# Two mixture-of-experts layers on one core: gate rows spread over the partitions by DMA instead of by a selector product on TensorE

## The reference

```python
def _L0_ffn_ref(...):
    shared = silu(xf @ Ws_up) @ Ws_down
    aff = xf @ centroids.T
    _, idx = top_k(aff + expert_biases, 8)
    w = sigmoid(take_along_axis(aff, idx, axis=1))
    w = w / (sum(w) + 1e-08)
    cw = zeros((T, E)).at[arange(T)[:, None], idx].add(w)   # the gates of layer 0
    h = silu(einsum('td,edf->etf', xf, W_up))
    y = einsum('etf,efd->etd', h, W_down)
    return shared + einsum('etd,te->td', y, cw)

def _L1_ffn_ref(...):
    probs = softmax(xf @ router_w.T)
    k_probs, k_idx = top_k(probs, 2)                        # normalised: the gates of layer 1
    # a token beyond an expert's capacity of int(1.25*N*2/8)+1 is dropped (gate 0)
    h = silu(buf @ w1); out = h @ w2                        # per expert
    return sum(out * gate) + x
```

## Time and profile before

| what | value |
|---|---|
| time, median of 3 runs | 1476.88 us (1471.17 to 1491.15) |
| the profiled execution's own time | 1489.87 us |
| its span | 1488.1 us |
| mean granted TensorE clock | 0.957 of full speed |
| PE busy | 1327.0 us, 89% |
| DVE busy | 1055.6 us, 71% |
| ACT busy | 949.4 us, 64% |
| POOL busy | 882.5 us, 59% |
| bytes read from HBM, written | 43.87 MB, 20.05 MB |

### The profile page before, as it was taken

How to read it: one execution, slowest core, us unless ns; L and a number is a source line. 1 busy time by engine, 2 the same in 40 slices (tenths; PEclk the granted TensorE clock), 3 DMA queues, 4 the chain that set the end, 5 groups by cost and what they waited for, 6 DMA issues and landing times. The chain is left out here.

```text
span 1488.1 us, 23328 instructions
## 1 busy us (share of the span) xinstructions
PE 1327.0 (89%) x6176; PEld 525.4 (35%) x6176; DVE 1055.6 (71%) x1843; ACT 949.4 (64%) x1732; POOL 882.5 (59%) x835
## 2 busy tenths in 40 slices
PE   2499898989889897599999999998999999999998
PEld 1223232322222221234444444443433444444443
DVE  6687887879787783577786786788878555455554
ACT  0055565757566576467767767766666777877776
POOL 2414342433433235467777777777777888878886
PEclk9997897989998899799999999999999999999999
DMA  2541523324252400431101001021110110001100
GB/s 60 86 68 41 78 56 57 74 38 91 35 83 51 65 5 9 124 94 29 40 9 40 27 29 40 8 85 34 57 37 8 37 29 26 13 21 29 30 7 8
DMA packets 92275, 65.36 MB, mean 44 GB/s; under 512 B 35786, under 2 KB 85900, under 8 KB 92172
## 3 DMA queue, kind: packets, MB, share of 16 engines
q1 hardware_dynamic: 91812, 63.91, 20.2%
q10 hardware_dynamic: 360, 0.30, 0.1%
HBM read 43.87 MB, written 20.05 MB: 43 GB/s over the span
## 5 line engine op out<-in xcount | busy, mean ns | idle before, releaser
L1266 POOL TENSOR_TENSOR m_hidl<-m_hid,m_hidh 128x512 f16<-128x512 f32 x520 | 613.3, 1185 | 212.2 <-ACT m_hidh L1311 188.8
L1534 DVE TENSOR_TENSOR m_hid<-m_silu,m_c 128x512 f32<-128x512 f32 x512 | 347.5, 684 | 247.7 <-ACT m_silu L1318 193.2
L588 ACT ACTIVATE a_probs<-a_score 128x512 f32<-128x512 f32 x512 | 293.8, 597 | 195.1 <-PE a_score L666 188.5
L1318 ACT ACTIVATE m_silu<-m_h 128x512 f32<-128x512 f32 x520 | 309.1, 595 | 131.1 <-PE m_h L1417 126.2
L1311 ACT ACTIVATE m_hidh<-m_hid 128x512 f16<-128x512 f32 x520 | 324.2, 624 | 90.8 <-DVE m_hid L1534 89.7
L762 DVE TENSOR_REDUCE a_mx<-a_mxps 128x2 f32<-128x1024 f32 x256 | 306.9, 1215 | 75.7 <-PE a_mxps L657 75.1
L666 PE MATMUL a_score<-a_qstack,a_kstack 74*128 74x512 bf16 x512 | 208.6, 412 | 21.3 <-DMA a_qstack<-a_mT 14.4
L657 PE MATMUL a_mxps<-a_kstack,a_qstack 72*128 72x512 bf16 x512 | 173.4, 424 | 43.2 <-DMA a_kstack<-t_parts 31.2
L1415 PE MATMUL m_h<-m_xh,m_wuh 128*128 128x512 f16 x520 | 198.8, 382 | 12.2 <-DMA m_rw<-rw 12.2
L1397 PE MATMUL m_y<-m_hidh,m_wdh 128*128 128x512 f16 x520 | 198.8, 382 | 2.5 <-ACT m_gT L1332 1.7
L1417 PE MATMUL m_h<-m_xh,m_wul 128*128 128x512 f16 x520 | 198.7, 382 | 0.0
(11 more groups left out here) (186 smaller groups left out, 1295.5 us busy)
## 6 DMA issues: line engine op xcount, KB each, us to landing
a_qstack<-t_parts SPq DMA_DIRECT2D x63, 128.0 KB
a_kstack<-t_parts SPq DMA_DIRECT2D x63, 128.0 KB
m_raw<-up SPq DMA_DIRECT2D x8, 512.0 KB, 3.9
m_raw<-down SPq DMA_DIRECT2D x8, 512.0 KB, 4.0
m_sT<-t_s SPq DMA_DIRECT2D x16, 256.0 KB, 3.4
t_parts<-a_qparts SPq DMA_DIRECT2D x24, 128.0 KB, 2.2
t_parts<-a_kparts SPq DMA_DIRECT2D x24, 128.0 KB, 2.3
a_xin<-x SPq DMA_DIRECT2D x8, 256.0 KB, 3.4
```

The costliest lines, as they stand in the source:

```text
L588: act.activation(probs[:, kt % 2, g, :], score[:, g % 2, :], ACT.Exp, scale=SCALE).then_inc(exp_done, 1)
L1266: pool.tensor_tensor(hidl[0:r0, k % r, :], hid[0:r0, k % r, :], hidh[0:r0, k % r, :], ALU.subtract).then_inc(lo_done, 1)
L1318: act.activation(silu[0:rows(q), k % RING[s.layer], :], hps[0:rows(q), k % 2, :], ACT.Silu, scale=1.0 / WS).then_inc(silu_done, 1)
L1534: dve.tensor_tensor(hid[:, k % r, :], silu[:, k % r, :], cps[:, (q // UPC[s.layer]) % 2, :], ALU.mult).then_inc(mul_done, 1)
```

## The change

The gates stay fp32 in DRAM (`cw0` 64 rows, `cw1` 8 rows). In both mixtures the selector product is gone: SP loads the row of each expert from DRAM straight to all partitions that need it, two rows per load (`GROUP`), into `gates`, a ring in SBUF of four groups, eight units in layer 0. In layer 0 a group takes two DMAs (one per half of the partitions, each 64 partitions x 2 rows x 2 KB) and serves two units; in layer 1 one DMA of 128 partitions x 2 rows serves eight units. DVE multiplies silu by the SBUF ring. A slot is refilled after its last product, also with the next stage's gates. The two PSUM banks that were `m_c` go to h, which has three in layer 0 and four in layer 1. The scaling by 64, which was the selector's, is in ACT's copy of cwT. The fp16 halves of the gates go (POOL L452, L455; DVE L1686, L1688), as do half the gate transposes in attention and three of four in layer 0; the selectors and the fp16 identity go as well. The loads of the weight chunks 4 to 9 move from ahead of the units into the units of the first stage.

```diff
+GROUP = 2
+GROUPS = UNITS // GROUP
+SLOTS = E1 // GROUP
+HBANKS = (3, 4)
...
-        cw = [sb(f"cw{p}", [P, TOK], F16) for p in range(2)]
+        gates = sb("gates", [P, SLOTS * GROUP, TOK])
...
-        cwhl = sb("cwhl", [P, TILES, 2, E1], F16)
-        cwT = sb("cwT", [2 * E1, TOK], F16)
-
-        hps = ctx.enter_context(nc.psum_tensor("m_h", [P, 2, 512], F32))
-        cps = ctx.enter_context(nc.psum_tensor("m_c", [P, 2, 512], F32))
+        cwT = sb("cwT", [TILES * E1, P])
+
+        hps = ctx.enter_context(nc.psum_tensor("m_h", [P, max(HBANKS), 512], F32))
...
+            def load_gates(s, g):
+
+                k = g % SLOTS
+                into = gates[:, GROUP * k:GROUP * k + GROUP, :]
+                if s.layer:
+                    sp.wait_ge(cw_out, Turn(0, s.i, s.p).n("cw_out", 16 * TILES))
+                    apart(sp)
+                    row = scratch["cw1"][GROUP * g:GROUP * g + GROUP, s.tokens()]
+                    sp.dma_start(into, row.unsqueeze(0).broadcast_to([P, GROUP, TOK])).then_inc(gate_in[k], 16)
+                    return
+                pair = scratch["cw0"].rearrange("(u a) t -> a u t", a=2)
+                for a in range(2):
+                    h = slice(a * (P // 2), a * (P // 2) + P // 2)
+                    row = pair[a, GROUP * g:GROUP * g + GROUP, s.tokens()]
+                    sp.dma_start(into[h], row.unsqueeze(0).broadcast_to([P // 2, GROUP, TOK])
+                                 ).then_inc(gate_in[k], 16)
...
             load_chunk(1)
+            for g in range(SLOTS):
+                load_gates(Turn(0, 0, 0), g)
             for dst, src in ((wg, "wg"), (bg, "bg"), (lnw, "lnw"), (lnb, "lnb"), (rw, "rw")):
...
             def unit(s, q):
+                if s.first() and q and 1 < (job_at(s, q - 1) or 0) < JOBS:
+
+                    j = job_at(s, q - 1) + 2
+                    sp.wait_ge(wsplit, 2 * (j - 1))
+                    load_chunk(j if j < JOBS else j + 1)
+                span = GROUP * (UPC[1] if s.layer else 1)
+                if q < UNITS and q % span == span - 1:
+
+                    g = q // span + SLOTS
+                    to = s if g < UNITS // span else s.following()
+                    if to:
+                        sp.wait_ge(mul_done, s.n("unit", q + 1))
+                        apart(sp)
+                        load_gates(to, g % (UNITS // span))
...
-                if not (s.first() and q < 2):
-                    pe.wait_ge(silu_done, s.n("unit", q - 1))
+                if not (s.first() and q < min(HBANKS)):
+                    pe.wait_ge(silu_done, s.n("unit", q - min(HBANKS) + 1))
...
-                if q < UNITS and q % UPC[n] == 0:
-                    c = q // UPC[n]
-                    if not (s.first() and c < 2):
-
-                        ago = (c - 1) * UPC[n] - (NQ[n] - UNITS if c < 2 else 0)
-                        if n and c < 2 and isinstance(s.i, int) and s.i == 0 and s.p == 0:
-                            ago = -1
-                        pe.wait_ge(mul_done, s.n("unit", ago))
-                    r = slice(0, 2 * (E0, E1)[n])
-                    pe.matmul(cps[:, c % 2, :], sel[n][:, c, :], cw[s.p][r], start=True, stop=True
-                              ).then_inc(c_done, 1)
...
-                if q < UNITS and q % UPC[s.layer] == 0:
-                    dve.wait_ge(c_done, s.n("c", q // UPC[s.layer] + 1))
+                if q < UNITS and q % (GROUP * UPC[s.layer]) == 0:
+                    g = q // (GROUP * UPC[s.layer])
+                    dve.wait_ge(gate_in[g % SLOTS], s.n("gate", 16 * (1 if s.layer else 2) * (g // SLOTS + 1)))
...
-                    dve.tensor_tensor(hid[:, k % r, :], silu[:, k % r, :], cps[:, (q // UPC[s.layer]) % 2, :],
+                    dve.tensor_tensor(hid[:, k % r, :], silu[:, k % r, :], gates[:, (q // UPC[s.layer]) % (SLOTS * GROUP), :],
                                       ALU.mult).then_inc(mul_done, 1)
```

More of the change, by code:

```diff
@@ L996, in back, with following @@
         return Turn(self.layer, self.i - 1, 1)
+    def following(self):
+        if self.p == 0:
+            return Turn(self.layer, self.i, 1)
+        if isinstance(self.i, int) and self.i == PASSES - 1:
+            return Turn(1, 0, 0) if self.layer == 0 else None
+        return Turn(self.layer, self.i + 1, 0)
     def after_next(self):
@@ L1032, in run_stages, with mixture_phase @@
         passes(eng, body)
[L1035 to L1049 removed]
+def mixture_phase(nc, io, scratch, ident):
     with ExitStack() as ctx:
@@ L1233, in follow @@
                     apart(sp)
-                    sp.dma_start(scratch["cw1"][:, b.tokens()], cwT[:]).then_inc(cw_out, 16)
+                    there = scratch["cw1"][:, b.tokens()].rearrange("e (t x) -> t e x", x=P)
+                    for t in range(TILES):
+                        sp.dma_start(there[t], cwT[E1 * t:E1 * t + E1]).then_inc(cw_out, 16)
                 if q == 31:
@@ L1317, in unit @@
                     act.wait_ge(mul_done, s.n("unit", q - min(RING) + 1))
-                act.activation(silu[0:rows(q), k % RING[s.layer], :], hps[0:rows(q), k % 2, :], ACT.Silu,
+                act.activation(silu[0:rows(q), k % RING[s.layer], :], hps[0:rows(q), k % HBANKS[s.layer], :], ACT.Silu,
                                scale=1.0 / WS).then_inc(silu_done, 1)
@@ L1484, in follow @@
                     elif name == "cwT":
[L1485 to L1489 removed]
+                        pe.wait_ge(dve_rel, b.n("dve_rel", DVE_USES.index("rank") + 1))
+                        op = pe.transpose(dst[0:TILES * E1, 0:P], cwcut[:].rearrange("p t e -> p (t e)"), ident[:])
                     elif name == "nT":
```

114 lines of the change are left out of this document (35 added, 79 removed).

## The result

| what | before | changed |
|---|---|---|
| time, median | 1481.66 us (4 runs, 1471.17 to 1491.15) | 1565.2 us (4 runs, 1559.66 to 1575.22) |
| ratio, 95% interval | | 1.0573 [1.0474, 1.0673] |
| the profiled execution: own time, span | 1489.87, 1488.1 us | 1575.22, 1573.5 us |
| mean granted TensorE clock | 0.957 | 0.943 |

The changed kernel is slower by 5.7%, some 85 us (0.0573 x 1482; 70 to 100 by the interval). Disturbed runs are left out of the ratios, so a ratio isn't just the quotient of two medians. The page's first part shows the order of the engines turned round: where PE led and DVE stood at 71%, DVE now leads.

The account below looks back on a forecast made before the run. PE was taken to bound the kernel, but DVE and POOL taking turns would bind after the change: +31 +81 +6 -1 = +117 us, giving 1594 us against the median; 8-in-10 range 1530 to 1675, the forecast's own 1535 to 1650.

Parts of the forecast that it names:

- The unit of 1.55 us: Mixture: hid and hidl take turns, 1.55 us a unit; seven plain layer-1 stretches grow 4.4 us each, +31.
- The eight stretches with follow-up work and the first: Mixture stages with follow-up work, plus the first with weight splits: +9 us each, nine times, +81; bounds -28 and +199.
- I take 69, near the upper one: Stretches with follow-up work: 69 us from 59.80, between 56.7 and 72.3, the latter if every hid waits a turn.
- The start of layer 0: Start of the mixture: eight gate loads ahead of rw on SP's queue delay PE by +6 us, bounds 3.8 and 7.4.
- PE's saving: Layer-1 stages: dropping eight selector products saves PE 3.3 us a stage, but no longer on the path.
- Gate loads afterwards: Mixture after the start: gate refills have cover, so their cost was taken as 0.
- Attention: Attention stages: fewer POOL casts, PE transposes and ACT copying, no selector building; taken as -1 us, bounds 0 and -3.
- 1 (no exclusion, 1397): Mixture: no exclusion for hid's product, or too rare to matter; 80 us off, 1397 us; chance 3%.
- 2 (paid by slack): Mixture: exclusion exists but slack pays; layer 1 +17, other stretches unchanged, start +4, 1498 us; chance 7%.
- 3 (1.85 a unit): Both layers: turns alternate badly, each instruction in full, 1.85 us a unit; 1780 us; chance 10%.
- 4 (gates late): Layer 0: gates arrive late, DVE waits for a DMA at each second unit; 1712 us; chance 5%.
- 5: Whole kernel: the change does not do what it says; called not likely, no size or percentage given.

Follow-up runs that it names:

- e1: The kernel before, with only hid's second input changed to a constant tile in SBUF, selector products and loads kept: 1588.98 us, ratio 1.0739.
- e2: The changed kernel with all gate loads and waits kept, but hid takes a constant from a PSUM bank of h: 1437.06 us, ratio 0.9666.
- e3: The changed kernel with correct gates from SBUF, but silu written in place into h's PSUM bank: 1440.28 us, ratio 0.9676.
- e4: The changed kernel with no gate load after the first eight, so later stages use wrong gates: 1576.01 us, ratio 1.0686.
- c2: The kernel before with the change's whole attention and nothing else of it: 1461.18 us, ratio 0.9906.
- e5: The changed kernel with the first eight gate loads moved behind the five small weights: 1564.91 us, ratio 1.0556.
- e6: e3 with the first eight gate loads moved behind the five small weights: 1444.8 us, ratio 0.9733.

## Why the prediction was right, and where its terms were off

The time forecast was 1594 us, the measured one 1565.2, in the forecast's own range and on its side. The mechanism is the one named: e1 makes it by itself, e2 and e3 take it away, e4 leaves it. In the profiles the three terms of the mixture sum to 112.5 us where I had 118. That this is so close is partly luck, as their misses of +4, -15 and +5 offset each other. The other part of the difference is attention, which I had at -1 and which came out at -14 by c2 and at -27 in the profiles. By its steps:

**The unit of 1.55 us.** Measured 1.565, by 0.55 and 1.01 for the two hand-overs, where I had 0.55 and 0.94 to 1.03 from the rows of the trace before. It holds in nearly all units: of 219 hids in the seven stretches 196 took about 1.6 us. Layer 1 came out at +35.3 against +31, 51.0 us in the stretch shown against 50.2. The unit gives 32 x 0.015 = 0.5 of these 0.8. The rest lies where a stage begins: there prod takes a whole turn (1.56 us from its start at 1266.53 to that of the next hid) where I had put 0.55, and a hid that finds POOL idle (0.68) gives part of that back. One sign was wrong as well: PE in layer 1 is busy for 92% (323.70 of 353.30), not 80 to 85%, in a view whose matmul ends are modelled.

**The eight stretches with follow-up work and the first.** +66.4 against +81. The first stage was as said, 74.6 - 65.7 = 8.9 against 9. The eight grew by 7.2 each, not 9. The step that failed is "I take 69, near the upper one", which let nearly every hid wait a turn. It was worked out on the stretch of 59.8 us, and this one became 66.3, +6.5. (That the eight have a mean of 68.4 is no support for the 69: their mean before was 61.2, not 59.8. The 39 instructions of POOL in the lower bound should have been 40, 0.2 us.) Of 198 hids from 733.0 to 1149.9, six of these stretches, 91 took 0.7 us. 75 of these found POOL idle when they started, and the other 16 a hidl within 0.06 us of its end; the 107 longer ones all started beside a busy POOL. A short one stands in the timeline of DVE at 851:

```profile
851.08 1.48 DVE L1535 TENSOR_TENSOR m_hid<-m_silu,m_gates 128x512 f32<-128x512 f32 x1
852.48 0.18 DVE L1683 SCALAR_TENSOR_TENSOR m_cwcut<-m_m,m_cwall 128x32 f32<-128x32 f32 x1
852.59 0.67 DVE L1535 TENSOR_TENSOR m_hid<-m_silu,m_gates 128x512 f32<-128x512 f32 x1
```

And of POOL at the same place:

```profile
849.74 2.27 POOL L1280 TENSOR_TENSOR m_hidl<-m_hid,m_hidh 128x512 f16<-128x512 f32 x2
853.30 4.29 POOL L1280 TENSOR_TENSOR m_hidl<-m_hid,m_hidh 128x512 f16<-128x512 f32 x3 [1.29 <-ACT m_hidh L1325]
```

The hid of 851.08 waited for the hidl that ended at 852.01, and ended 0.55 behind it. After DVE's other work POOL had nothing in store, so it now sat idle for 1.29 us, until hidh of that hid was ready, and the next hid, at 852.59, ran alone in 0.67. In the stretch of 66.3 us hid has a mean of 1079 ns, not the 1550 of the bound, and hidl 1352, by its groups:

```profile
L1280 POOL TENSOR_TENSOR m_hidl<-m_hid,m_hidh 128x512 f16<-128x512 f32 x32 | 42.8, 1352 | 15.4 <-ACT m_hidh L1325 14.0 <-PE m_y L1413 1.2
L1535 DVE TENSOR_TENSOR m_hid<-m_silu,m_gates 128x512 f32<-128x512 f32 x33 | 35.1, 1079 | 5.7 <-ACT m_silu L1332 5.7
```

DVE's other work stayed what it was, 58.03 - 35.1 = 22.9 us (22.7 before). Charging only those hids at which POOL has a hidl in store gives DVE's busy time, 58.0 us, but not yet the stretch: for 8.3 of the 66.3 us DVE stood idle, 5.7 of them ahead of a hid, for silu.

**The start of layer 0.** +10.8 against +6, outside the bounds of 3.8 to 7.4. The step that failed is the issue, "8 at 0.43 to 0.48". The timeline of SP:

```profile
575.19 7.82 SPq L1166 DMA_DIRECT2D m_gates<-t_cw  x8
583.06 1.49 SPq L1192 DMA_DIRECT2D m_wg<-wg  x1
584.59 1.62 SPq L1192 DMA_DIRECT2D m_bg<-bg  x1
586.25 1.47 SPq L1192 DMA_DIRECT2D m_lnw<-lnw  x1
587.76 0.76 SPq L1192 DMA_DIRECT2D m_lnb<-lnb  x1
588.56 0.43 SPq L1192 DMA_DIRECT2D m_rw<-rw  x1
```

The eight gate loads took 7.82 us to issue, and the four small weights ahead of rw 5.34 in place of 4 x 0.43 = 1.72, even bg with its 2 KB, while the DMA share was 0.95. With the load of m_cw gone (0.43) that is 7.82 + 3.62 - 0.43 = 11.0 us; rw itself landed 4.5 us after its issue, 4.7 before. So all of the +10.8 is issue. Two things were wrong in my term: a gate load takes 0.60 us to issue even later (the median of its 256), not 0.43 to 0.48, and of the first eight the last two took 1.59 and 1.49. I had taken a value between issue and transfer; in fact the issues became slower than either estimate. That e5 and e6 got little or nothing back for it was not foreseen.

**PE's saving.** 3.3 us per layer-1 stage off the path, by the prediction. It was off the path, and it is 2.8 to 3.0 where it is on it (e2, e3).

**Gate loads afterwards.** 0, and e4 shows next to nothing: 620.8 against 621.8.

**Attention.** -1 with bounds 0 and -3; measured -14 (-5 to -23) by c2. The step that failed priced two transposes by their own time; what the runs show in its place is a shorter wait for a load (14.4 and 3.2 us) and a higher granted clock in the seventh stage, with the cause open. Put together, 35.3 + 66.4 + 10.8 - 14 = +98.5, at the upper edge of the measured 70 to 100; with the profiles' own -27 it is +85.

**The rivals.** 1 (no exclusion, 1397) would not have come out even without exclusion: e2 and e3 are at 1437 and 1440. It counted PE's 7 us in each of the nine stretches, and e3's nine gained 555.4 - 539.8 = 15.6 in all. In e2's stretch of layer 0 PE is busy for 50.94 of 57.90 us, so it isn't PE alone that sets the time there; which wait does was not followed up. 2 (paid by slack) fell with the measured +35 and +66. 3 (1.85 a unit) fell: the turns alternate at 1.565. By the Trainium skill's page "SBUF — State Buffer", section "SBUF: two separate sides", the lock is held for the whole instruction and the other engine blocks. The trace agrees that they exclude each other, but 1.565 us a unit is less than 0.69 + 1.16, so part of the waiting instruction's time passes meanwhile. By the section "Who interferes with whom" of the same page of the Trainium skill, a DVE instruction with at most one SBUF input, outside the modes that use both ports, does not contend with GpSimd. e2 and e3 agree for hid: one PSUM input is enough to avoid the turns. 4 (gates late) fell with e4. 5 did not happen.

## What to carry to other kernels

Before moving an operand of a DVE instruction from PSUM to SBUF, see whether that leaves it with both inputs in SBUF while POOL is busy on SBUF tiles. If so, find one instruction of this kind in the trace, once beside a busy and once beside an idle POOL, and price the pair by the two hand-overs. Charge it only where POOL has work at that moment, and add the time in which the engine is idle anyway. If there is a choice, leave either input in PSUM: here that turned +5.7% into -3.2%.
